# A two-pass graph kernel: first row strip in one transfer, other filler work on TensorE, twelve low parts of z on GpSimd, and work lists in another order

## The reference

```python
a    = (adj + adj.T) * 0.5 + eye(2048)
deg  = sum(a, axis=1)
dinv = where(deg > 0, deg ** -0.5, 0)
y    = (adj @ (dinv[:, None] * a * dinv[None, :])) @ x
r    = x + y
out  = (r - mean(r)) / sqrt(var(r) + 1e-5)      # per row
```

## Time and profile before

| | |
|---|---|
| median of 3 runs | 376.9 us (376.05 to 379.38) |
| profiled execution | 377.6 us |
| span of its instructions | 375.8 us |
| TensorE busy / VectorE / ScalarE / GpSimd | 364.0 / 251.0 / 116.3 / 2.1 us |
| mean granted TensorE clock | 0.997 of full speed |
| moved by DMA | 46.95 MB |

### The profile page before, as it was taken

One profiled execution on the slowest core, in us unless ns is written; L12 is line 12 of the kernel. 1 busy time (PEld: TensorE's weight loads), 2 busy tenths in 40 slices (PEclk: granted clock), 3 DMA queues, 4 the chain that ended last, 5 costly groups with the idle time before them and its releaser, 6 DMA issues.

```text
span 375.8 us, 4351 instructions
## 1 busy us (share of the span) xinstructions
PE 364.0 (97%) x1643; PEld 301.0 (80%) x1643; DVE 251.0 (67%) x485; ACT 116.3 (31%) x188; POOL 2.1 (1%) x8
## 2 busy tenths in 40 slices
PE   7999999899999999999999999999999999999993
PEld 6888886688888888888888888888888888888882
DVE  1697898998989899877399327534455454445564
ACT  2583353232134214332466222122122212221210
POOL 1000000000000000010000000000000000000000
PEclk9999999999999999999999999999999999999998
DMA  7999999999999996210001001301111011111102
GB/s 226 345 199 298 208 277 205 308 195 233 263 296 195 204 246 240 88 36 0 30 7 50 2 0 56 113 0 56 58 57 55 16 42 56 58 56 56 56 33 82
DMA packets 70309, 46.95 MB, mean 125 GB/s; under 512 B 59408, under 2 KB 61456, under 8 KB 68368
## 3 DMA queue, kind: packets, MB, share of 16 engines
q1 hardware_dynamic: 70288, 46.67, 50.6%
HBM read 42.47 MB, written 4.19 MB: 124 GB/s over the span
## 4 chain that ended last, share of the span: by engine, by line
PE 80%; SPq 14%; DMA 3%; DVE 1%; issue 1%; ACT 0%; DVEq 0%; ACTq 0%
PE bank L950 15%; PE bank L949 15%; PE bank L951 15%; SPq L252 10%; PE bank L888 8%; PE bank L892 8%; PE bank L896 8%; PE bank L911 3%; PE bank L908 3%; PE bank L905 3%; DMA XZ<-in_x 2%; DMA AT<-in_adj 2%; SPq L265 1%; SPq L276 1%; SPq L271 1%
## 5 line engine op out<-in xcount | busy, mean ns | idle before, releaser
L949 PE MATMUL bank<-UH,ATH 128*128 128x512 f32 x256 | 99.6, 389 | 0.0
L950 PE MATMUL bank<-UL,ATH 128*128 128x512 f32 x256 | 99.6, 389 | 0.0
L951 PE MATMUL bank<-UH,ATL 128*128 128x512 f32 x256 | 99.6, 389 | 0.0
L807 DVE TENSOR_TENSOR ATL<-AT,ATH 128x1024 fp32r<-128x1024 f32 (+2 forms) x48 | 40.3, 867 | 76.6 <-ACT ATH L413 76.6
L413 ACT ACTIVATE ATH<-AT 128x1024 fp32r<-128x1024 f32 (+2 forms) x48 | 37.1, 805 | 85.0 <-PE bank L951 81.3
L378 ACT ACTIVATE SH<-strip 128x1024 fp32r<-128x1024 f32 (+2 forms) x48 | 37.4, 814 | 62.7 <-PE bank L896 37.8
L949 PEld LDWEIGHTS bank<-UH,ATH 128*128 128x128 f32 x256 | 48.0, 188 | 10.1
L951 PEld LDWEIGHTS bank<-UH,ATL 128*128 128x128 f32 x256 | 48.0, 188 | 10.1
L950 PEld LDWEIGHTS bank<-UL,ATH 128*128 128x128 f32 x256 | 48.0, 188 | 9.8
L888 PE MATMUL bank<-ZH,SH 128*128 128x512 f32 x168 | 41.8, 391 | 1.8 <-ACT ZH L385 1.8
L605 DVE TENSOR_TENSOR SL<-strip,SH 128x1024 fp32r<-128x1024 f32 (+2 forms) x48 | 39.8, 858 | 4.4 <-ACT SH L378 4.4
(11 more groups left out here) (43 smaller groups left out, 227.9 us busy)
## 6 DMA issues: line engine op xcount, KB each, us to landing
strip<-in_adj SPq DMA_DIRECT2D x15, 1024.0 KB, 7.3
AT<-in_adj SPq DMA_DIRECT2D x56, 256.0 KB, 6.6
XZ<-in_x SPq DMA_DIRECT2D x18, 256.0 KB, 6.5
xr<-in_x SPq DMA_DIRECT2D x16, 256.0 KB, 2.7
out<-outr SPq DMA_DIRECT2D x16, 256.0 KB, 2.0
col<-in_adj SPq DMA_DIRECT2D x4, 512.0 KB, 7.1
strip<-in_adj SPq DMA_DIRECT2D x4, 256.0 KB, 7.5
```

The source lines that it names most:

```text
L807: ins = nc.vector.tensor_tensor(half_place(ATL[i % 2], lo, hi, len(src.shape)), src, high.bitcast(F32), ALU.subtract)
L949: nc.tensor.matmul(bank[:, :], wh, UH[:, k, :], start=opens and n == 0, stop=False)
L950: nc.tensor.matmul(bank[:, :], wh, UL[:, k, :], start=False, stop=False)
L951: last = nc.tensor.matmul(bank[:, :], wl, UH[:, k, :], start=False, stop=ends)
```

## The change

- The first strip comes in one transfer of 1 MB, issued after the second column piece, where four transfers of 256 KB were interleaved with the column pieces.
- The filler transposes between the column pieces are 9, 32 and 2, where they were 9, 9 and 9.
- ZL of z 4, 5 and 8 to 17 is made on GpSimd by two instructions (XZ times dinv in place, then minus ZH), where VectorE made each with one. TensorE waits for them on a semaphore of their own.
- The lists of SyncE, ScalarE and VectorE stand in another order, and the blocks of tiles 12 to 15 are issued after a wait for step 15, behind x 11, which itself waits for step 16.

The core of the diff:

```diff
+    POOL_Z = (4, 5, 8, 9, 10, 11, 12, 13, 14, 15, 16, 17)
...
             for n in range(CHUNKS):
-                rows = slice(n * CW, (n + 1) * CW)
-                load_columns(0, rows, colpiece_in[n])
-                sp.dma_start(strip[STRIP_SLOT[0]][:, rows], adj[0:P, rows]).then_inc(rowpiece_in[n], 16)
+                load_columns(0, slice(n * CW, (n + 1) * CW), colpiece_in[n])
+                if n == 1:
+                    load_strip(0)
             load_strip(1)
+            load_x(1)
             load_x(0)
-            load_x(1)
-            load_x(2)
+            load_block(2, 1)
             load_block(2, 0)
-            load_block(2, 1)
             load_strip(2)
             load_strip(3)
+            load_x(2)
             load_x(3)
...
             load_strip(9)
-            load_x(10)
             load_block(10, 1)
             load_strip(10)
             load_x(9)
             load_strip(11)
+            load_x(10)
+            load_x(11)
+            sp.wait_ge(prod_done, step_end(Z_LAST[7]))
             load_block(12, 0)
-            load_x(11)
             load_block(12, 1)
             load_block(14, 1)
             load_strip(12)
-            load_block(14, 0)
             load_strip(13)
             load_x(12)
             load_x(13)
+            load_block(14, 0)
...
+            def z_low(k):
+
+                t, slot = Z_TILES[k], z_slot(k)
+                pool.wait_ge(zh_done, k + 1)
+                nc.gpsimd.tensor_scalar(XZ[slot][:, :], XZ[slot][:, :], dinv[:, t:t + 1], 1.0, ALU.mult, ALU.mult
+                                        ).then_inc(x_scaled, 1)
+                pool.wait_ge(x_scaled, POOL_Z.index(k) + 1)
+                nc.gpsimd.tensor_tensor(ZL[slot][:, :], XZ[slot][:, :], ZH[slot][:, :].bitcast(F32), ALU.subtract
+                                        ).then_inc(late_zl_done, 1)
+
+            z_low(4)
...
+            z_low(17)
+
             pool.wait_ge(dinv_ready, NB)
...
             sum_rows(2)
             add_diagonal(3)
+            turn(3, 0)
+            sum_rows(3)
             degree_reciprocal(2)
             degree(2)
-            sum_rows(3)
+            degree_reciprocal(3)
...
+            def wait_for_z_low(k):
+                if k in POOL_Z:
+                    pe.wait_ge(late_zl_done, POOL_Z.index(k) + 1)
+                else:
+                    pe.wait_ge(zl_done, sum(j not in POOL_Z for j in range(k + 1)))
+
...
-                    busy(9, banks[7])
+                    busy((9, 32, 2)[n], banks[7])
```

More of the change, by code:

```diff
@@ L541, in wait_for_strip @@
             def wait_for_strip(t):
-                if t == 0:
-                    dve.wait_ge(rowpiece_in[0], 16)
-                else:
-                    slot = STRIP_SLOT[t]
-                    dve.wait_ge(strip_in[slot], 16 * sum(STRIP_SLOT[j] == slot for j in range(1, t + 1)))
+                slot = STRIP_SLOT[t]
+                dve.wait_ge(strip_in[slot], 16 * sum(STRIP_SLOT[j] == slot for j in range(t + 1)))
             def sum_rows(t):
@@ L635, in _ @@
             degree_reciprocal(0)
+            add_diagonal(1)
             degree(0)
-            add_diagonal(1)
             sum_rows(1)
@@ L645, in _ @@
             s_low(2)
-            s_low(3)
-            turn(3, 0)
-            turn(2, 0)
             turn(2, 1)
             turn(3, 1)
+            s_low(3)
+            turn(2, 0)
             add_diagonal(2)
@@ L685, in _ @@
             sum_rows(6)
-            z_low(5)
+            add_diagonal(7)
             degree_reciprocal(6)
-            add_diagonal(7)
             degree(6)
@@ L697, in _ @@
             turn(8, 0)
-            turn(9, 0)
             add_part(2, 0)
@@ L705, in _ @@
             add_part(2, 5)
+            turn(9, 0)
+            add_part(2, 6)
+            add_diagonal(8)
+            add_part(2, 7)
             turn(8, 1)
-            add_part(2, 6)
-            add_part(2, 7)
             s_low(13)
+            sum_rows(8)
             turn(9, 1)
-            add_diagonal(8)
             s_low(14)
-            sum_rows(8)
+            degree_reciprocal(8)
+            add_diagonal(9)
             turn(10, 0)
-            turn(11, 0)
-            degree_reciprocal(8)
-            s_low(15)
-            add_diagonal(9)
             degree(8)
             sum_rows(9)
+            s_low(15)
+            turn(11, 0)
+            s_low(16)
+            degree_reciprocal(9)
             turn(10, 1)
-            turn(11, 1)
-            z_low(8)
-            degree_reciprocal(9)
             add_diagonal(10)
-            s_low(16)
             degree(9)
             sum_rows(10)
-            z_low(9)
+            turn(11, 1)
             degree_reciprocal(10)
-            s_low(17)
             add_diagonal(11)
             degree(10)
+            s_low(17)
             sum_rows(11)
-            z_low(10)
             degree_reciprocal(11)
+            degree(11)
             s_low(18)
-            degree(11)
             s_low(19)
-            z_low(11)
             turn(12, 0)
-            add_part(3, 0)
+            turn(13, 0)
             s_low(20)
-            add_part(3, 1)
-            add_part(3, 2)
+            for b in range(HB):
+                add_part(3, b)
+            s_low(21)
+            turn(12, 1)
             turn(13, 1)
-            add_part(3, 3)
-            add_part(3, 4)
-            add_part(3, 5)
-            add_part(3, 6)
-            add_part(3, 7)
-            turn(14, 1)
-            turn(12, 1)
-            s_low(21)
+            s_low(22)
             add_diagonal(12)
-            s_low(22)
-            turn(13, 0)
             sum_rows(12)
             add_diagonal(13)
+            turn(15, 1)
+            s_low(23)
             degree_reciprocal(12)
-            s_low(23)
+            degree(12)
             sum_rows(13)
-            z_low(12)
-            degree(12)
-            add_diagonal(14)
-            turn(15, 0)
+            turn(14, 1)
             degree_reciprocal(13)
-            z_low(13)
             s_low(24)
@@ L771, in _ @@
             turn(14, 0)
-            z_low(14)
+            add_diagonal(14)
+            turn(15, 0)
             sum_rows(14)
+            s_low(25)
+            degree_reciprocal(14)
             add_diagonal(15)
-            degree_reciprocal(14)
-            s_low(25)
-            turn(15, 1)
             degree(14)
             sum_rows(15)
-            z_low(15)
             degree_reciprocal(15)
+            degree(15)
             s_low(26)
-            degree(15)
             s_low(27)
-            z_low(16)
             add_part(4, 0)
+            add_part(4, 1)
             s_low(28)
-            add_part(4, 1)
             add_part(4, 2)
```

104 lines of the change are left out of this document (58 added, 46 removed).

## The result

The changed kernel took 375.0 us as the median of 14 runs (374.2 to 376.0); the kernel before, run beside it, 378.5 us (375.8 to 379.8). The ratio is 0.9915 with a 95% interval of 0.9894 to 0.9936: 3.2 us less by the ratio, 3.5 by the medians. The forecast was 376.3 in a range of 374.5 to 378.9. The profiled execution took 375.02 us, its span 373.2; 1.8 us lie outside, as before.

The account below looks back on a forecast made before the run. Bound: transfer queue up to some 75 us, TensorE after it. Terms 1.76 - 0.25 - 0.85 = 0.65 us off the profiled 377.6 give 376.95, as a median 376.3; own range 375.4 to 377.2, full range 374.5 to 378.9.

Parts of the forecast that it names:

- sign of being wrong: Wrong would be TensorE unbroken from 60 us on (gain 3 us or more), or ZL waits at each of steps 16 to 19.
- the hole at the start closes: Rival: low transfer rate at 4 to 6 us goes, all landings come 1.3 us earlier, 375.0 us; chance 0.15.
- What bounds the kernel: Transfer queue up to some 75 us, TensorE after it; 3.8 us lost in steps 0 to 9 are all to gain.
- First strip: Start of kernel: one transfer makes step 0 0.8 us late (bounds -0.6 and +1.3), at no cost on the path.
- x 5 and step 9: x 5 lands at 66.5 to 67.1, step 9 begins about 67.9; step 10 at 74.3, gain 1.76 us.
- 0.25 us for ZL of z 6: Step 10: low part of z 6 ends at 76.3, wanted at 76.1, costing 0.25 us with the restart.
- Strip 8: Step 12: strip lands at 88.8, its add is done at 89.7, wanted at 90.2; costs nothing, 0.5 us cover.
- GpSimd: price: Twelve low-part pairs on GpSimd at 1.75 us each (0.65 plus 1.1), with VectorE and GpSimd blocking each other.
- new wait of 0.85 us: Step 19: SL there at 124.8, wanted at 123.95, so TensorE waits 0.85 us, partly at ZL of z 10.
- The rival's rule: Rival, GpSimd becomes the bound: each us on a pair costs 4 us at steps 15 to 19; chance 0.22.
- Blocks 12 to 15, halved dinv: Blocks go out some 10 us later, halved dinv comes near 185 us; both cost nothing, without cover some 1 us each.
- Filler: Filler transposes at the start can win nothing, as the granted clock is 1.00 even while TensorE idled, 7 to 8 us.

Follow-up runs that it names:

- second experiment: Kernel before with only x 4 to x 6 moved forward and dinv of tile 4 ahead of the turn: 377.6 us, ratio 0.999 [0.995, 1.003].
- run of both: Kernel before with first strip in one transfer, x 4 to x 6 and dinv of tile 4 moved, low part of z 5 early: 374.9 us, ratio 0.9913.

## Why the prediction was right, and where it was not

The time lay in the range and within 1%, but under the forecast's own range of 375.4 to 377.2. Of the mechanism, the prediction's own sign of being wrong came true: TensorE unbroken from 60 us on and a gain of 3 us or more. None of the waits it named (for ZH of z 6, and at steps 18 and 19) was there. The number is that of the rival "the hole at the start closes", 375.0 with a chance of 0.15; but of that rival only the closing of the hole is shown, not that all landings come earlier by it. That 376.3 is as near as it is, is in part luck: the base was 1.6 us too low (376.9 against 378.5) and the saving 2.8 us too small (0.65 against 3.5 by the medians), and the two errors offset each other.

- **What bounds the kernel: right.** Transfers up to 75 us, TensorE behind them, 3.8 us to win. The change won 2.6 of these in its profile, all ahead of step 10.
- **First strip: the choice failed; what the closed hole is worth stays open.** "Against: column pieces are as before" took the pieces of 256 KB between them for harmless. With them the stretch from 4 to 5 us moved 84 to 115 GB/s in all four profiles, without them 335 to 407 in all ten. The lead is 0.40 MB at 6 us by the stretches of the change and of before, and gone at 24 us; with the hole, x 5 still landed at 64.4 in the second experiment. Undoing the single transfer alone did take the gain away by the median, but in its profile through step 0 and step 6. The lateness of step 0, 0.8 forecast, was 1.02. It was to cost nothing because step 4 would begin near 40.6 even with step 0 on time. That cover was not there: where step 0 began at 18.14 and 18.50, step 4 began at 40.02 and 40.34, at TensorE's pace, and in the change TensorE runs unbroken from step 0 on. So in that execution the lateness counted in full, as the prediction said it would without the cover; a start 1.45 us earlier met waits in step 5 and ahead of step 10.
- **x 5 and step 9: right in kind, too small.** x 5 landed at 64.45 (66.5 to 67.1 forecast), since its queue was earlier besides; the base was late, too, for in the second profile of the unaltered kernel before x 5 landed at 67.8, not 69.4. The chain computed behind it (sums of tile 6 at 69.7, ZH of z 6 from 73.45) ran 2.0 us ahead of that: 67.66 and 71.36. It therefore stopped being the limit; step 10 at 73.45 instead of 74.3 is the pace of TensorE. The 0.25 us for ZL of z 6 fell away with it (done at 74.31, wanted at 75.27). That the move alone would give 1.76 is refuted: alone it gave 0.999 [0.995, 1.003], and in its profile the low part of z 5, behind the turns, cost 1.7 us at step 9. Taking ZL of z 5 out from behind the sums of tile 6 (onto GpSimd in the change, ahead of them on VectorE in the run of both) was a part of the move; the prediction took only its 0.7 us on VectorE.
- **Strip 8: right.** Issued at 81.69, it was there at 86.8, ahead of need.
- **GpSimd: price near, consequence mis-sized.** 0.70 + 1.30 us alone where 0.65 + 1.1 were taken. Half of the 0.30 fixed and the rest by columns and inputs, as the prediction says, would have been 0.75 + 1.35, which is nearer. With the mutual blocking a pair took 2.8 on average in the run (15.1 and 18.3 us for twelve of each). Each engine waits for the other, as assumed (3.39 and 3.21 us above). **The new wait of 0.85 us did not come:** strip 9 landed at 95.5 instead of 97.9, and the way from there to SL of step 19 took 25.9 us where 26.9 were counted. There was 1.4 us of room. The rival's rule, 4 us for each on a pair at steps 15 to 19, met the size and not the place: 1.31 us a pair cost 5.1 us, where the rule less the room gives 3.8, and half of the waits lay behind step 20.
- **Blocks 12 to 15, halved dinv: nothing, as said.** The halving ended at 182.9.
- **Filler: the reason was wrong, the sum is open.** That the granted clock is 1.00 even where TensorE does nothing was read from a stretch of 1 us; an idle time of 2.68 us did bring it down. In that profile step 0 and the last start came 0.6 us later; the times of the runs neither show nor exclude that much.
- **The base: too coarse.** The forecast was laid against a median of three runs, 376.9; with 14 to 31 runs in a session it is 378.0 to 378.5. The predicted saving was 0.65 us, the measured 3.5 by the medians; of the difference some 2.0 us show in the two profiles (2.6 against 0.65), and 0.9 is that the profiled execution of before, 377.6, lay below the median of its later runs, 378.5, and not above it as the prediction took it.

## What to carry to other kernels

Where a queue of transfers sets the pace for the first tens of microseconds, look for stretches with few bytes at its start before you count what each move gains: one large transfer in place of four small ones closed such a stretch here. Then follow the bytes onward before you call it the gain: the lead was gone 18 us later, and the run that would show what it is worth by itself is missing. After a move, ask for the last part that the step wants: x 5 came early, and step 9 still waited 1.7 us for its low part. Run the kernel before several times ahead of trusting its median or its one profile, since x 5 landed 1.6 us apart in two executions of one and the same kernel.

## What the hardware showed beyond that

- GpSimd and VectorE instructions with two inputs held each other up even for tiny work: 0.21 us became 1.20 for a multiply of one column with two inputs beside a subtraction of 512 columns. Transposes, with one input, ran beside it unharmed (1.23 us at 109.15 while a subtraction ran from 109.63 to 110.93), and the addition of the diagonal behind them took 0.72 instead of 0.27 and ended 0.15 us after the subtraction. The Trainium skill, page SBUF — State Buffer, section Who interferes with whom, states that a VectorE instruction with two SBUF inputs contends with a GpSimd instruction that reads SBUF; the trace agrees, in both directions (1.20 for 0.21 on VectorE, 3.21 for 1.30 on GpSimd).
- A subtraction of two 512-column inputs took GpSimd 1.30 us, a scaling with one input 0.70.
- The granted clock fell to 0.50 (1.2 GHz) behind idle times of TensorE of 2.68 and 4.61 us, and stayed at 1.00 (2.4 GHz) behind 2.16 and 1.82.
